# Edge network: one of 32 source tiles assembled by single-column copies in place of a gather

## The reference

```python
h = maximum(layernorm(x), 0)
x = x + relu(segment_sum(norm[e] * h[dst[e]], src) @ W.T + b)     # first layer
h = maximum(layernorm(x), 0)
edge = concat([h[src], h[dst], edge_attr])                        # 48 + 48 + 16 features per edge
m = relu(relu(edge @ W1 + b1) @ W2 + b2) @ W3 + b3                # hidden width 128
x = x + h + segment_sum(m, dst) / max(count(dst), 1)              # "h +": the layer adds its own input
```

## Time and profile before

| | |
|---|---|
| time, median of 3 runs | 7111.28 us |
| lowest and highest run | 7111.13, 7126.65 us |
| profiled execution: span from its first to its last instruction | 6161.4 us |
| the profiled execution's own time beside its span | not given by the page |
| median run less the span | 949.9 us |
| granted clock of TensorE, mean over the span | 0.909 |
| busy in the span: TensorE, VectorE, ScalarE, GpSimd | 5105.3, 3550.1, 1709.0, 4073.1 us |
| instructions recorded | 148,527 |

### The profile page before, as it was taken

How to read it: one execution, slowest core, us unless ns; L and a number is a source line. 1 busy time by engine, 2 the same in 40 slices (tenths; PEclk the granted TensorE clock), 3 DMA queues, 4 the chain that set the end, 5 groups by cost and what they waited for, 6 DMA issues and landing times. The chain is left out here.

```text
span 6161.4 us, 148527 instructions
## 1 busy us (share of the span) xinstructions
PE 5105.3 (83%) x40298; PEld 4259.0 (69%) x40299; DVE 3550.1 (58%) x11415; ACT 1709.0 (28%) x3091; POOL 4073.1 (66%) x3903
## 2 busy tenths in 40 slices
PE   4885999999999768778888877787787888888877
PEld 4883899999999656666666666666666666666666
DVE  8998999999996643443434434434344343434444
ACT  3336666666663321111111111111111111111110
POOL 0106667666664467777777777777777777777776
PEclk9998999999999888888888888888988888888888
DMA  9206999999999733333333333333333333333332
GB/s 165 32 0 161 278 289 288 288 291 290 290 291 271 177 107 83 83 85 83 85 83 83 85 84 83 85 83 84 84 83 85 83 84 84 84 84 84 83 85 66
DMA packets 653787, 816.43 MB, mean 133 GB/s; under 512 B 426282, under 2 KB 471052, under 8 KB 653114
## 3 DMA queue, kind: packets, MB, share of 16 engines
q1 hardware_dynamic: 478251, 592.65, 32.8%
q0 software_dynamic: 175360, 221.63, 17.0%
HBM read 563.36 MB, written 250.47 MB: 132 GB/s over the span
## 5 line engine op out<-in xcount | busy, mean ns | idle before, releaser
L1729 POOL DMA_INDIRECT p_got<-p_tab,idx_d x3128 | 2962.5, 947 | 964.4 <-issue 864.2
L1715 ACT ACTIVATE h<-z,b_col 128x512 f32<-128x512 f32 x782 | 537.6, 687 | 3391.9 <-PE z L1855 3343.6
L1719 DVE TENSOR_TENSOR h<-z,nb 128x512 f32<-128x512 f32 x782 | 540.9, 692 | 1606.3 <-PE z L1695 1598.6
L1689 PEld LDWEIGHTS z<-ident_f,p_got 128*128 128x128 f32 x3128 | 415.8, 161 | 1385.5 <-DMA p_got<-p_tab,idx_d 1239.8
L1689 PE MATMUL z<-ident_f,p_got 128*128 128x128 f32 x3128 | 596.9, 323 | 784.9 <-DMA p_got<-p_tab,idx_d 784.7
L1073 PE MATMUL a_ps<-tile_r,pair_l 128*128 128x288 fp8e5 x5280 | 1041.4, 287 | 75.4 <-DVE tile_r L1160 45.5
L910 POOL DMA_INDIRECT sum_tab<-val_s,idx_s x496 | 788.9, 1590 | 466.9 <-ACT val_s L1027 332.5
L1094 PE MATMUL out_ps<-gw,a_got 121*128 121x144 bf16 x11340 | 1076.4, 225 | 4.5 <-DMA a_got<-a_tab 4.2
L1695 PEld LDWEIGHTS z<-w_sb,h 128*128 128x128 f32 x6256 | 1033.5, 234 | 56.4
L1695 PE MATMUL z<-w_sb,h 128*128 128x128 f32 x6256 | 1023.6, 318 | 0.0
L1036 ACT CAST stage<-a_ps 128x576 uint16<-128x576 f32 x1320 | 838.6, 640 | 405.0 <-PE a_ps L1073 397.4
(11 more groups left out here) (202 smaller groups left out, 3692.9 us busy)
## 6 DMA issues: line engine op xcount, KB each, us to landing
a_tab<-stage SPq DMA_DIRECT2D x330, 576.0 KB
a_got<-a_tab SPq DMA_DIRECT2D x330, 576.0 KB
rel<-rel_row SPq DMA_DIRECT2D x391, 192.0 KB
p_got<-p_tab,idx_d POOLq DMA_INDIRECT x3128
ef<-in_edge_t SPq DMA_DIRECT2D x391, 64.0 KB
q_win<-q_tab SPq DMA_DIRECT2D x782, 24.0 KB
src_bc<-src_row SPq DMA_DIRECT2D x124, 128.0 KB
a_tab<-big SPq DMA_DIRECT2D x22, 472.5 KB
```

Of the source, the lines that this page charges most:

```text
L1689: pe.matmul(out_tile, p_rows[:, j, :], ident_f[:, :], start=False, stop=False, is_transpose=True, skip_group_check=True)
L1729: pool.indirect_dma_start(p_rows[:, j, :], None, p_tab, bass.IndirectOffsetOnAxis(idx[:, j:j + 1], 0)).then_inc(landed, 16)
```

## The change

One tile in 32 is no longer gathered. OWN = (0,): in slot 0 of each eight groups, from group 8 on, tile 3 of 4 is left out of `gather`, and TensorE makes its source part itself, as `w1a_sb` (the source part of W1) times `h_col`, a tile whose 128 columns are the `h` of the 128 source nodes. For this

- the node stage's ScalarE copies each transposed block once more, into `h_all` (48 x 12672 f32), which takes the place of the accumulator in `big`;
- the first stage also writes `own_row`, a table with the source indices of these tiles as 2-byte numbers, one row of 128 for a tile;
- SP loads a row of it into `own_idx`, two groups after the slot's last use;
- in four steps out of eight, VectorE and ScalarE each load 2 x 8 of the indices into registers (`nodes_of`) and later in the same step copy 16 columns of `h_all` into `h_col` (`columns`), 128 columns in all. VectorE loads after `keep_h2` and copies at the end of its step; ScalarE loads before it waits for z1 and copies after `make_h1`;
- TensorE waits for `cols_made` before the matmul.

`seg_acc` becomes a tile of its own, cleared by VectorE and ScalarE at the start of the edge network, and `cnt_acc` moves to partition 64 of `big`, so the transpose of the counts takes the third block of rows. VectorE's `load_base` moves ahead of the transpose. In the short stage's `sum_by_node` and in the last stage only operands' shapes and the number of semaphores change.

The diff, its core:

```diff
+OWN = (0,)
+OWN_TILE = GROUP - 1
+QUARTERS = 4
+LOT = 8
...
+    own_row = dram("own_row", [OWNS, P], U16)
...
-seg_acc = big[:, 0:NPP]
+h_all = big[0:F, 0:NPP]
+CNT_AT = 2 * SPAN
+cnt_acc = big[CNT_AT:CNT_AT + 1, 0:NPP]
...
+        sp.dma_start(own_row.rearrange("(c p) e -> p c e", p=OWN_ROWS), own_s[:, :, :]).then_inc(tables_set, 16)
...
+        act.copy(own_f, src_i[:, :].rearrange("p (m t) -> p m t", t=OWN_STEP * GROUP)[:, :, OWN_TILE])
...
+        act.copy(own_s[:, :, :], own_ps[:, :, :]).then_inc(ids_copied, 1)
...
+                wait_past(act, h_t_ready, 2 * (k - 2))
                 act.copy(h_t[0:F, :, :], t_ps_c[:, 0:CB, :]).then_inc(h_t_ready, 1)
+                act.wait_ge(h_t_ready, 2 * (k - 2) + 1)
+                act.copy(h_all[:, (k - 2) * CB * P:(k - 1) * CB * P],
+                         h_t[0:F, :, :].rearrange("p c n -> p (c n)")).then_inc(h_t_ready, 1)
...
-        pool.wait_ge(agg_ready, NK)
-        pool.memset(seg_acc, 0.0).then_inc(t_zero, 1)
-        pool.wait_ge(t_zero, 4)
...
-def src_part(pe, z1, p_rows):
-
-    for j, out_tile in enumerate(each_tile(z1)):
-        pe.matmul(out_tile, p_rows[:, j, :], ident_f[:, :], start=False, stop=False, is_transpose=True,
+def src_part(pe, z1, p_rows, tiles=range(GROUP)):
+
+    for j in tiles:
+        pe.matmul(each_tile(z1)[j], p_rows[:, j, :], ident_f[:, :], start=False, stop=False, is_transpose=True,
...
-def gather(pool, p_rows, idx, landed):
-    for j in range(GROUP):
+def gather(pool, p_rows, idx, landed, tiles=range(GROUP)):
+    for j in tiles:
...
+        def owned(q, s):
+            return s in OWN and past(q, DEPTH)
+
+        def gathered_tiles(q, s):
+            return [j for j in range(GROUP) if j != OWN_TILE or not owned(q, s)]
...
+        def building(q, s):
+
+            for b, slot in enumerate(OWN):
+                k = (s - slot - 1) % DEPTH
+                after = DEPTH - 1 - k
+                if k < QUARTERS and (not isinstance(q, int) or DEPTH <= q + after < NE):
+                    yield b, slot, k, after
+
+        def nodes_of(engine, b, first):
+
+            return [nc.values_load_multi_w_load_instructions(
+                own_idx[b][0:1, at:at + LOT], engines=[engine], min_val=0, max_val=N - 1,
+                skip_runtime_bounds_check_because="they are the sources of edges, each below N")[1]
+                for at in (first, first + LOT)]
+
+        def columns(copy, b, first, nodes):
+
+            for lot in range(2):
+                for i, node in enumerate(nodes[lot]):
+                    at = first + lot * LOT + i
+                    last = copy(h_col[b][0:F, at:at + 1], h_all[:, bass.ds(node, 1)])
+                last.then_inc(cols_made[b], 1)
...
+                    sp.dma_start(w1a_sb[0:F, :], w1ab[:, 0:H]).then_inc(w_loaded, 16)
+                for b, slot in enumerate(OWN):
+                    use = q + (DEPTH - 2)
+                    if s == (slot + 2) % DEPTH and (not isinstance(q, int) or DEPTH <= use < NE):
+                        sp.wait_ge(cols_made[b], (q + (DEPTH - 2 - slot)) * 2)
+                        sp.sem_inc(sp_turns, 1)
+                        row = use // OWN_STEP if isinstance(q, int) else sp.snap(
+                            nc.s_assert_within(use // OWN_STEP, 0, OWNS - 1))
+                        sp.dma_start(own_idx[b][:, :], own_row[bass.ds(row, 1), :]).then_inc(own_loaded[b], 16)
...
-                gather(pool, p_got[s % UNROLL], half_of(idx[s // 2], s), gathered[s % UNROLL])
+                gather(pool, p_got[s % UNROLL], half_of(idx[s // 2], s), gathered[s % UNROLL], gathered_tiles(q, s))
...
+                lots = []
+                for b, slot, k, after in building(q, s):
+                    if k == 0:
+                        act.wait_ge(own_loaded[b], (q + (after - slot)) * 2)
+                        act.sem_inc(any_turn, 1)
+                    first = (2 * k + 1) * 2 * LOT
+                    lots.append((b, first, nodes_of(mybir.EngineType.Activation, b, first)))
                 act.wait_ge(z1_made, q + 1)
 
                 wait_past(act, z2_made, q - 1)
                 make_h1(act, h1[s % 2], z1[s % 2]).then_inc(h1_ready, 1)
-
+                for b, first, nodes in lots:
+                    columns(act.copy, b, first, nodes)
+
+            act.copy(seg_acc[:, SEG_CUT:], zero_b[:, 0:1].to_broadcast([P, NPP - SEG_CUT])).then_inc(cnt_zero, 1)
+            for b in range(len(OWN)):
+                act.sem_inc(cols_made[b], COLS)
+            act.wait_ge(ef_zero, 2)
...
-                pe.wait_ge(gathered[s % UNROLL], in_slot(q, s % UNROLL, UNROLL, 16 * GROUP))
-                src_part(pe, z1[k], p_got[s % UNROLL])
+                pe.wait_ge(gathered[s % UNROLL], rows_landed(q, s))
+                src_part(pe, z1[k], p_got[s % UNROLL], gathered_tiles(q, s))
+                if owned(q, s):
+                    b = OWN.index(s)
+                    pe.wait_ge(cols_made[b], (q + (COLS - s)) * 2)
+                    pe.sem_inc(pe_turns, 1)
+                    pe.matmul(each_tile(z1[k])[OWN_TILE], w1a_sb[:, :], h_col[b][:, :], start=False, stop=False,
+                              skip_group_check=True)
...
+            pe.wait_ge(w_loaded, 16 * (W_LOADS + 1))
...
+                    dve.wait_ge(cnt_zero, 16 + 2)
 
                 wait_past(dve, seg_added, q)
-                dve.transpose(cnt_row[:, :], cnt_col[s][0:SPAN, :]).then_inc(cnt_turned, 1)
+                first = load_base(dve, q)
+                dve.transpose(cnt_row[CNT_AT:QR, :], cnt_col[s][CNT_AT:QR, :]).then_inc(cnt_turned, 1)
                 dve.wait_ge(seg_made, q + 1)
-                first = load_base(dve, q)
-                at, count = seg_acc[:, bass.ds(first, SPAN)], cnt_acc[0:1, bass.ds(first, SPAN)]
+                at, count = seg_acc[:, bass.ds(first, SPAN)], cnt_acc[:, bass.ds(first, SPAN)]
                 dve.tensor_tensor(at, at, seg_ps[s % 2][:, :], ALU.add)
                 dve.wait_ge(cnt_turned, q + 1)
-                dve.tensor_tensor(count, count, cnt_row[0:1, :], ALU.add).then_inc(seg_added, 1)
-
+                dve.tensor_tensor(count, count, cnt_row[CNT_AT:CNT_AT + 1, :], ALU.add).then_inc(seg_added, 1)
...
+            dve.memset(seg_acc[:, 0:SEG_CUT], 0.0).then_inc(cnt_zero, 1)
...
+                lots = []
+                for b, slot, k, after in building(q, s):
+                    if k == 0:
+                        dve.wait_ge(own_loaded[b], (q + (after - slot)) * 2)
+                        dve.sem_inc(any_turn, 1)
+                    first = 2 * k * 2 * LOT
+                    lots.append((b, first, nodes_of(mybir.EngineType.DVE, b, first)))
                 if past(q, 2):
                     add_segment(q - 2, (s - 2) % UNROLL)
+                for b, first, nodes in lots:
+                    columns(dve.tensor_copy, b, first, nodes)
```

More of the change, by code:

```diff
@@ L201, in build_gnn @@
     src_row = dram("src_row", [SG, W], U16)
+    OWN_STEP = DEPTH // len(OWN)
+    OWNS = NG // OWN_STEP
+    assert OWN == tuple(range(0, DEPTH, OWN_STEP)) and OWN_STEP >= QUARTERS and P == QUARTERS * 4 * LOT
+    assert max(g for g in range(NE) if g % DEPTH in OWN) * GROUP + OWN_TILE < EDGES // P
+    own_row = dram("own_row", [OWNS, P], U16)
     g_tab = dram("g_tab", [NPP, PLANES * F], BF16)
@@ L636, in _ @@
                 for c in range(SG * GROUP // TURNED):
-                    last = pe.transpose(turned_ps[:, c, :], src_s[:, c * TURNED:(c + 1) * TURNED], ident_f[:, :])
+                    pe.transpose(turned_ps[:, c, :], src_s[:, c * TURNED:(c + 1) * TURNED], ident_f[:, :])
+                for c in range(OWNS // OWN_ROWS):
+                    last = pe.transpose(own_ps[:, c, :], own_f[:, c * OWN_ROWS:(c + 1) * OWN_ROWS], ident_f[:, :])
                 last.then_inc(turned, 1)
@@ L1703, in sum_by_node @@
             for j in range(GROUP):
-                last = pe.matmul(seg_ps[0:1, nodes:2 * nodes], ones_b[:, :], hot_c[:, j, :], start=(j == 0),
-                                 stop=(j == GROUP - 1))
+                last = pe.matmul(seg_ps[:, nodes:2 * nodes], ones_b[:, :].to_broadcast([P, P]), hot_c[:, j, :],
+                                 start=(j == 0), stop=(j == GROUP - 1))
             return last
@@ L1744, in build_gnn @@
             cnt_col = [sb(f"cnt_col{s}", [QR, SPAN], F32, life) for s in range(UNROLL)]
-            cnt_row = sb("cnt_row", [SPAN, SPAN], F32, life)
+            cnt_row = sb("cnt_row", [QR, SPAN], F32, life)
+            w1a_sb = sb("w1a_sb", [P, H], F32, life)
+            h_col = [sb(f"h_col{b}", [P, P], F32, life) for b in range(len(OWN))]
+            own_idx = [sb(f"own_idx{b}", [1, P], U16, life) for b in range(len(OWN))]
             hot_t = [sb(f"hot_t_d{k}", [QR, W], BF16, life) for k in range(2)]
@@ L1769, in build_gnn @@
                 gathered = [sem(f"gathered{s}", ctx) for s in range(UNROLL)]
+                own_loaded = [sem(f"own_loaded{b}", ctx) for b in range(len(OWN))]
```

(23 more changed lines are left out.)

55 lines of the change are left out of this document (31 added, 24 removed).

## The result

The changed kernel takes 7557.81 us (median of 4 runs, 7539.78 to 7575.73), the kernel before in the same comparison 7112.31 us: a ratio of 1.063 (1.061 to 1.065). It is 446 us slower, where 106 us faster was forecast; the time lies outside the range, 348 us above its upper end.

The account below looks back on a forecast made before the run. The prediction took GpSimd's gather, one indirect DMA every 1.25 us, as the bound. It summed -121 (97 gathers) + 10 (port lock) + 6 (small edits) = -105 us, from 7111 to 7006 us; range 6985 to 7210 us.

Parts of the forecast that it names:

- the loads: In VectorE's building step, two loads of 8 register values take 1.7 us, between bounds of 0.61 and 4.9.
- the cover: VectorE's time to spare in a turn of eight groups, 4.75 us; gone at a building step of 6.7 us.
- rival A: Register loads are paid by the value, 4.2 us a step, and VectorE becomes the bound: 7515 us; chance 0.21.
- The building step: VectorE's step with column loads and copies, four in eight: 2.0 + 1.7 + 1.8 = 5.5 us.
- The hold: VectorE's copies and GpSimd's descriptor work exclude each other for some 0.3 us; 0.6 us a building step.
- the lock: VectorE's copies delay GpSimd's gathers at the shared port, 0.1 us a turn of eight groups, +10 us.
- Rival B: The port lock falls on GpSimd's gathers: 7462 us in full, chance 0.02; in part, still faster, 0.10.
- The turn: Eight edge-stage groups take the larger of 38.75 us and 4 building steps + 12; that is 34, so hidden.
- 97 gathers: Gathers removed from GpSimd in the edge stage, at 1.25 us each: 121 us less.
- The rest: Small edits in the node, edge, first and last stages: +6 us in sum (0 to 20).
- ScalarE: hidden: ScalarE's 16 copies, loads of 1.7 us and activation, together 4.0 us (to 5.3) a step, delay no one.
- The base of the sum: The 949.9 us between the 6161.4 us span and the 7111.28 us run lie outside recorded instructions, unchanged.

Follow-up runs that it names:

- e11: The changed kernel, loads and copies spread over 7 steps, 4 columns a step on VectorE, 14 or 15 on ScalarE: 7431.24 us, 1.0465 of before.
- e7: The changed kernel with ScalarE's register loads alone; VectorE loads none and copies fixed columns, all copies stay: 6047.24 us, 0.9811 of before.
- e8: The changed kernel with VectorE's register loads alone; ScalarE loads none and copies fixed columns, all copies stay: 6461.36 us, 1.0480 of before.
- e5: The changed kernel with all register loads, but one copy, from a loaded address, for each lot of 8: 6045.21 us, 0.9808 of before.
- e6: The changed kernel with all 3128 gathers, no own-tile matmul, no register loads, one fixed-column copy a lot: 6168.93 us, 1.0011 of before.
- e18: The same kernel as e6, timed again in another comparison: 6172.96 us, 1.0011 of before.
- e17: The changed kernel, loads and copies spread over 6 steps, own tile's index row loaded later: 6046.09 us, 0.9800 of before.
- comparisons 2 and 5: Sets of runs timed beside the unchanged kernel before, on chips 11 and 12; it takes 6163.56 us in 2 and 6164.81 us in 5.
- e1: The kernel before, unchanged, profiled once more: 7111.29 us, with a span of 7109.5 us.
- e15: The same kernel as e8, timed again in another comparison: 7643.06 us, 1.0678 of before.
- e16: The changed kernel itself, timed again beside e15: 7668.59 us, 1.0711 of before.
- e4: The changed kernel without register loads, with all its copies, from fixed columns: 7043.51 us, 0.9901 of before.
- e2: The changed kernel without register loads and with one fixed-column copy for each lot of 8: 6962.40 us, 0.9795 of before.
- e12: The same kernel as e2, timed again in another comparison: 6963.24 us, 0.9813 of before.

## Why the prediction was wrong, step by step

**The term that failed: the loads.** The prediction took 1.7 us for two loads, the geometric middle of 0.61 and 4.9. They take 3.65 us on VectorE, 3.23 of them visible in a late step. Its own limit was 2.9 us for the cover and 3.2 for the gain. The middle was chosen because the load is one instruction with 16 bytes of data; loads of 1, 4 and 8 values take 0.305, 0.959 and 1.826 us there (e11, the changed kernel), some 0.22 us more for each value, so it is paid by the value. That was rival A's mechanism. The Trainium skill ("Runtime: NRT & Kernel Launch", Instruction fetch mechanics) states about 200 ns a register even in bulk, for loads from HBM. The traces agree, with 0.23 and 0.21 us from SBUF. The prediction's estimate by that page is 3.4 us and 7205 us; 16 x 0.2 gives 3.2 us, by its own sum 7127 us, and where the other 0.2 comes from it doesn't say.

**The building step.** Forecast 5.5 us, measured 7.09: loads +1.5, plain work 2.2 in place of 2.0, copies 1.66 in place of 1.8. The hold did not come: no one-column copy takes more than 149 ns, although 0.39 was seen for one of 12 columns. The gathers stay at a median of 944 ns and are busy for 2870.7 and 2870.9 us in e7 and e8, which have all the copies, and 2870.2 in e5, so the +10 us for the lock finds nothing to answer to. Rival B falls. The Trainium skill ("SBUF — State Buffer", Who interferes with whom) states that a VectorE copy in a two-port mode contends with GpSimd. No effect of that shows here for one-column copies.

**The turn.** The rule "the larger of 38.75 and 4 building steps + 12" puts its limit at 6.7 us. The runs lie on both sides as it says: under it 38.8 us a turn (e5 and e7, whose building steps are 6.3 and 5.2 us in the mean), over it the gain is lost (e8). But above the limit it is too mild. With late steps of 7.09 us it gives 40.4 us, 1.6 over the gathers' pace; e8's turn is 4.3 over it. So even with the right price of a load the rule would have found only some 160 of the 416 us between e5 and e8.

Two things are missing in it. The first building step of a turn is no late step: it takes 9.0 us, 2.0 more. And the other four steps are 3.0 us only in part of the turns. In the building steps TensorE waits for one-hots, 2.6, 2.0, 1.7 and 0.6 us in a turn, and between these waits part of its matmuls are at the lower of its two clock levels, 1.2 and 2.4 GHz. In 33 of the 94 turns counted it is back at the upper one as VectorE catches up; there the other four steps are 2.7 us in the mean, and the turn is 41.0. In the other 61 the lower level lasts into the catching up, VectorE waits longer for z2 (2.91 us in the row below), the four steps are 3.5 us, and the turn is 44.3. One stretch of each kind, by windows (the clock is the third number from the end, as a share of 2.4 GHz), and the wait in the first:

```profile
4233.00:4238.00 5.00, 5.00 (x19) 3.86 (x19) 3.55 (x13) 0.42 (x1) 3.60 (x4) 0.50 0.38 98
4323.00:4328.00 5.00, 5.00 (x34) 3.89 (x34) 4.05 (x13) 0.69 (x1) 3.78 (x5) 1.00 0.38 98
```

```profile
4240.37 0.69 DVE L1744 TENSOR_TENSOR h<-z,nb 128x512 f32<-128x512 f32 x1 [2.91 <-PE z L1720]
```

Over the edge stage the granted clock is a mean of 0.76 of full speed in e8 and 0.90 in e5. That the lower level goes with turns 3.3 us longer is counted in the trace; no run changed the clock alone.

**The gain and the rest.** 97 gathers: 121 us forecast, 123.7 measured (e6 less e5). The view behind the earlier trace rows has one more line, `PE z L1855: 88.1, 289`: gaps of the same 0.305 us under z1's name, so that the reading of 1.25 us a gather stands. The rest: 6 us forecast, 5.4 and 8.1 measured (e6, e18). ScalarE: hidden, as forecast (e7), though its building step has 5.7 us of work in place of 4.0, loads of 3.43 in place of 1.7. Sum of all this, where before takes 6165 us and VectorE's work is in six steps of about half the load: 105 us forecast, 119 measured (e17).

**The base of the sum.** "All outside the first and last recorded instruction" was wrong. The span of 6161.4 us belongs to an execution of about 6164 us, as in comparisons 2 and 5; the runs of 7111 us spend the 950 us inside the span, 876 of them in the edge stage (e1), where the gather does not set TensorE's pace. There the loss has the same main cause, shown in one comparison: with VectorE's loads alone the kernel stands 484 us above before, the changed kernel 510 (e15 and e16). Copies that are free in comparison 2 cost 81 us there (e4 less e2), and the 6-step kernel, which gains 2.0% in the one, loses 0.65% in the other.

**Rival A's number.** It gave 7515 us, 43 below the result, by a turn of 44 us. In comparison 2, on whose kind of trace it was worked out, VectorE's part is a turn of 43.1. That its sum is near the result is in part luck: its loads of 4.2 us and building step of 8.0 were too long by 0.5 and 0.9 us, the turn's rule too mild, and the base another: the changed kernel has a turn of 53.6 us there, from 49.0.

**What stays open.** What delays TensorE's results where before takes 7100 us, and why the same kernels meet it in one comparison and not in another; the chip is one candidate. Other queues are uneven there too, as VectorE's register arithmetic for the copies shows, first in the changed kernel on record, then in e8 (minimum, median, maximum in ns):

```profile
L1856 DVEq FUSED_REGOPS  x6208: 2/46/1391, 2287.4 to 7480.8; - x194
```

```profile
L1859 DVEq FUSED_REGOPS  x6208: 46/46/53, 2217.7 to 6388.2; - x194
```

With it stays open why 97 gathers fewer are worth 2% there as well (e2, e12), though TensorE hardly waits for a gather: the small edits alone were measured only where before takes 6165. The changed kernel itself was not measured there; e8, with its VectorE unchanged and ScalarE's part free by e7, says about 1.048.

## What to carry to other kernels

Price a register load by its values, 0.2 us or more each in these traces, and add it to the step of the engine that executes it: work off the bound is free only up to the step at which that engine feeds the bound late. Count the steps of a turn one by one: the first heavy one, which no lateness hides, was 2 us longer here than the next, and the waits that it caused went with a slower TensorE just when it had to catch up. Then spread the work, so that no step passes the pace, and look at what else waits for its end (here SyncE's reload held back all loads behind it). Set a profile's span beside the timed runs before making a sum on it: here a gap of 13% was time of another kind of execution, not a fixed cost outside the span.

## What the hardware showed that was not expected

A load of 8 two-byte values from SBUF takes 1.826 us on VectorE and 1.713 on ScalarE, one of 4 takes 0.959 on VectorE (e11). Copies of one 48-value column start some 0.10 us apart on VectorE with an address from a register (16 in 1.68 us), with 46 ns of register arithmetic for each, and 0.06 apart from a fixed address (16 in 1.05 us, e7); no copy was longer than 149 ns on VectorE, and the gathers beside them stayed at 944 ns. The same program took 6164 and 7106 us in two comparisons, on two chips.
